# Nodes 4p to 4p+3 of a block on partition p: x and out in runs of 1 KB, turns that read every fourth column, and four changes of order

## The reference

```python
# layer 0: e = par * (diag * x @ W) + x, with one set (u) for nodes 0..2047 and one (i) for the rest
h = adj @ (adj.T @ e)
x = _layernorm(x + (layernorm(h) * gamma + beta + x))
# layer 1
x = _layernorm(x + (1.0 - 0.1 * x - 0.01 * sum(x * (adj @ x), axis=1)))
# layer 2
deg = clip(sum(adj, axis=1) + 1.0, 1.0, None)
z = concatenate([x, (adj @ x + x) / deg]) @ W + b
x = _layernorm(x + relu(z) / max(norm(relu(z)), 1e-12))
# layer 3
T1 = L @ x; T2 = 2 * L @ T1 - x; T3 = 2 * L @ T2 - T1      # L is adj
x = _layernorm(x + x @ w[0] + T1 @ w[1] + T2 @ w[2] + T3 @ w[3] + bias)
```

## Time and profile before

| | us |
|---|---|
| median of 3 runs | 1488.62 (1487.05 to 1488.67) |
| the profiled execution, its own time | 1490.14 |
| its span | 1487.5 |
| PE busy | 1471.7 (99%) |
| DVE busy | 612.6 (41%) |
| ACT busy | 257.5 (17%) |
| DMA queue of SP, share of 16 engines | 90.1% |

### The profile page before, as it was taken

The page is one execution under the profiler, slowest core; times in us unless marked ns, Lnnn a source line. Parts: engine busy times, 40 slices in busy tenths (PEclk is TensorE's granted clock), DMA queues, the critical chain, the costliest instruction groups (busy, mean ns, idle before and its releaser), DMA issues.

```text
span 1487.5 us, 17128 instructions
## 1 busy us (share of the span) xinstructions
PE 1471.7 (99%) x6422; PEld 683.8 (46%) x6422; DVE 612.6 (41%) x1274; ACT 257.5 (17%) x535; POOL 61.3 (4%) x66
## 2 busy tenths in 40 slices
PE   8999999999999999999999999999999999999997
PEld 5555555555555543334444344444444434444332
DVE  5756565655555568424222653325111031100532
ACT  3433434343433320000100000100000010000210
POOL 0000000000000002100000011000000000000010
PEclk9999999999999999999999999999999999999999
DMA  9999999999999998999888698776487879888998
GB/s 306 392 414 417 416 414 405 387 415 392 390 416 401 389 397 330 421 420 421 303 296 302 277 365 315 283 269 257 150 287 286 299 295 354 299 301 306 395 421 321
DMA packets 121632, 517.86 MB, mean 348 GB/s; under 512 B 20396, under 2 KB 20436, under 8 KB 71636
## 3 DMA queue, kind: packets, MB, share of 16 engines
q1 hardware_dynamic: 119664, 516.46, 90.1%
q10 hardware_dynamic: 1892, 0.35, 0.1%
HBM read 410.61 MB, written 106.17 MB: 347 GB/s over the span
## 4 chain that ended last, share of the span: by engine, by line
issue 99%; POOLq 0%; POOL 0%; DVE 0%
POOL power_out L541 0%; POOLq L539 0%; POOLq L541 0%; DVE rows L1046 0%; POOL ident L534 0%; POOLq L536 0%; POOL ident L536 0%; POOLq L1308 0%
## 5 line engine op out<-in xcount | busy, mean ns | idle before, releaser
L855 PE MATMUL ps_u<-blk,vectors 128*128 128x512 f32 (+1 forms) x1904 | 681.4, 593 | 1.3 <-DMA blk<-a_transposed 1.1
L855 PEld LDWEIGHTS ps_u<-blk,vectors 128*128 128x128 f32 (+1 forms) x1904 | 274.8, 170 | 368.4 <-issue 362.3
L580 ACT ACTIVATE blk<-ps_turn 128x512 f32<-128x512 f32 x400 | 201.9, 625 | 331.0 <-PE ps_turn L665 317.2
L1222 DVE TENSOR_TENSOR part<-part,ps_u 64x512 f32<-64x512 f32 (+1 forms) x40 | 27.4, 686 | 447.6 <-PE ps_u L855 447.0
L710 PE MATMUL ps_h<-blk,u_rows 128*64 128x512 f32 x720 | 164.4, 599 | 0.0
L957 DVE TENSOR_REDUCE row_part<-blk 128x4 f32<-128x2048 f32 x68 | 152.4, 2278 | 0.1
L941 DVE TENSOR_TENSOR part<-part,ps_h 128x512 f32<-128x512 f32 x80 | 55.0, 687 | 184.3 <-PE ps_h L710 184.3
L693 PE MATMUL ps_u<-blk,e 128*64 128x512 f32 x544 | 125.3, 600 | 0.1
L665 PEld LDWEIGHTS ps_turn<-ident,blk 128*128 128x128 f32 x1040 | 113.5, 141 | 19.5 <-issue 19.5
L665 PE MATMUL ps_turn<-ident,blk 128*128 128x128 f32 x1040 | 120.6, 274 | 0.0
L541 POOL TENSOR_TENSOR power_out<-power_in,minus_half 128x4 f32<-128x4 f32 x60 | 60.6, 1010 | 1422.6 <-DVEq L1009 1422.6
(11 more groups left out here) (119 smaller groups left out, 621.5 us busy)
## 6 DMA issues: line engine op xcount, KB each, us to landing
blk<-a_transposed SPq DMA_DIRECT2D x276, 1024.0 KB, 6.2
a_transposed<-blk SPq DMA_DIRECT2D x100, 1024.0 KB, 13.4
blk<-in_adj SPq DMA_DIRECT2D x65, 1024.0 KB, 11.9
nat_far<-in_adj SPq DMA_DIRECT2D x32, 1024.0 KB, 11.8
early_blk<-a_transposed SPq DMA_DIRECT2D x12, 1024.0 KB, 8.1
blk<-in_adj SPq DMA_DIRECT2D x12, 256.0 KB, 6.3
nat_far<-a_transposed SPq DMA_DIRECT2D x2, 1024.0 KB, 12.1
rows<-in_x SPq DMA_DIRECT2D x10, 128.0 KB, 8.2
```

The source lines that it names most:

```text
L580: nc.scalar.activation(blk[:, n % RING, t, :], ps_t[t][:, :], ACT.Copy)\
L855: mm = pe.matmul(acc, left, tiles[:, t, :], start=first, stop=last)
L1222: V.tensor_tensor(part[parts, cols], part[parts, cols], ps_both[r % 2][parts, :], ALU.add)\
```

## The change

Partition p now holds nodes 4p to 4p+3 of a block, tile c node 4p + c. x and out then lie in memory as one run of 1 KB per partition and block, where they were four of 256 bytes. A tile of adj is still 128 runs of 2 KB, but the four of a partition are neighbouring rows. So that a turned block has its contraction in the same order, the transposes of adj and of u (`every_fourth`) read 128 columns that lie 16 bytes apart. diag comes as 10 rows of 512, is multiplied by par on its 10 partitions before it is turned, and par goes to those 10 partitions only. The order changes in these places: x of block 1 is loaded and turned after the first quarter of block 1; first_e goes behind the third quarter; times_w(1) goes ahead of u_part(0); e(1) is made ahead of the first row sum; W_i is issued one block later; turn_h(3), (7) and (9) and the addition for e = 3 go earlier; diagonal blocks in sweep 4 go ahead of the last block of row 6; the addition of (5, 4) goes into the root wait of row 3.

```diff
-    a_blocks = adj.rearrange("(t p) j -> p t j", p=P)
-    x_rows = x.rearrange("(t p) f -> p t f", p=P)
-    out_rows = out.rearrange("(t p) f -> p t f", p=P)
+    a_blocks = adj.rearrange("(i p c) j -> p i c j", p=P, c=TB)
+    x_rows = x.rearrange("(i p c) f -> p i c f", p=P, c=TB)
+    out_rows = out.rearrange("(i p c) f -> p i c f", p=P, c=TB)
...
+    RUN_BEFORE_END = {2: HEAD[2] + 2, 4: 6}
+    SOON_TURNED, SOON_ADDED = {(1, 1): 3}, {0: 1, 1: 3}
+    TURNED_TWO = (6, 8)
...
-                    if s == LATE_HEAD and r == head + 2:
+                    if r == RUN_BEFORE_END.get(s):
...
+        def every_fourth(row, t):
+            return row.rearrange("p (q t) -> p t q", t=TB)[:, t, :]
...
-                if n < NB:
-                    tiles = slice(n * TB, (n + 1) * TB)
-                    sp.dma_start(rows[:, tiles, :], x_rows[:, tiles, :]).then_inc(x_loaded[n], 16)
+                tiles = slice(n * TB, (n + 1) * TB)
+                if n < NB and n != 1:
+                    sp.dma_start(rows[:, tiles, :], x_rows[:, n]).then_inc(x_loaded[n], 16)
                 if n < IN_QUARTERS:
                     for c in range(TB):
-                        sp.dma_start(nat(n)[:, c, :], a_blocks[:, n * TB + c, 0:BLK])\
+                        if n == 1 and c == 1:
+                            sp.dma_start(rows[:, tiles, :], x_rows[:, n]).then_inc(x_loaded[n], 16)
+                        sp.dma_start(nat(n)[:, c, :], a_blocks[:, n, c, 0:BLK])\
...
-            const(diag_flat[0:UT, :], diag_u.rearrange("(t p) -> t p", p=P))
-            const(diag_flat[UT:NT, :], diag_i.rearrange("(t p) -> t p", p=P))
+            const(diag_flat[0:UB, :], diag_u.rearrange("(i q) -> i q", q=BLK), diag_loaded)
+            const(par[0:UB, :], par_u.partition_broadcast(UB), diag_loaded)
+            const(diag_flat[UB:NB, :], diag_i.rearrange("(i q) -> i q", q=BLK), diag_loaded)
+            const(par[UB:NB, :], par_i.partition_broadcast(NB - UB), diag_loaded)
             for h in range(2):
                 const(w0[half(h), 0, h, :], w_u)
-            const(par[:, 0, :], par_u.partition_broadcast(P), par_u_loaded)
-            const(par[:, 1, :], par_i.partition_broadcast(P), par_i_loaded)
...
-                        mm = pe.transpose(ps_t[t][:, c * P:(c + 1) * P], nat(n)[:, c, t * P:(t + 1) * P],
+                        mm = pe.transpose(ps_t[t][:, c * P:(c + 1) * P], every_fourth(nat(n)[:, c, :], t),
                                           ident[:, :])
...
-                    mm = pe.transpose(ps_u[j % 2][:, t * P:(t + 1) * P], u_turned[:, t * P:(t + 1) * P], ident[:, :])
+                    mm = pe.transpose(ps_u[j % 2][:, t * P:(t + 1) * P], every_fourth(u_turned[:, :], t), ident[:, :])
...
             def first_u():
+                times_w(1)
                 u_part(0)
-                times_w(1)
 
             turn_x_in(0)
-            turn_quarters(0, {1: first_e})
-            turn_x_in(1)
-            turn_quarters(1, {1: first_u})
+            turn_quarters(0, {2: first_e})
+            turn_quarters(1, {0: lambda: turn_x_in(1), 1: first_u})
...
-                if e > 0:
+                if e > 0 and e not in SOON_TURNED.values() and e - 1 not in TURNED_TWO:
                     turn_h(e)
+                    if e in TURNED_TWO:
+                        turn_h(e + 1)
...
-            def weigh_diag(k, tiles):
-                V.tensor_tensor(par_prod[:, k:k + 1], par[:, k, 0:1], par[:, k, 1:2], ALU.mult)
-                dve.drain()
+            def weigh_diag():
+                dve.wait_ge(diag_loaded, 16 * N_DIAG)
+                V.tensor_tensor(par_prod[:, :], par[:, 0:1], par[:, 1:2], ALU.mult)
+                dve.drain()
+                V.tensor_scalar(diag_flat[:, :], diag_flat[:, :], par_prod[:, 0:1], None, ALU.mult)
+                dve.drain().then_inc(diag_weighed, 1)
                 dve.wait_ge(diag_turned, 1)
-                V.tensor_scalar(diag[:, tiles], diag_in[:, tiles], par_prod[:, k:k + 1], None, ALU.mult)
+                V.tensor_copy(diag[:, :].rearrange("p (i c) -> p c i", c=TB),
+                              diag_in.rearrange("p (c i) -> p c i", c=TB))
                 dve.drain()
...
+                if soon is not None:
+                    soon()
                 V.tensor_tensor(out_rows_centred[r % 2][:, :, :], ta[:, :, :], over_rows(mean_var[:, :, 0]), ALU.subtract)
...
-                if e + 2 < NB:
+                if e + 2 < NB and e + 2 not in SOON_ADDED.values():
                     add_last_h(e + 2)
...
+                        elif s == SWEEPS - 1 and r == 3:
+                            ENDS[s](i, n, soon=lambda: add_y(s, 4))
```

More of the change, by code:

```diff
@@ L112, in build @@
         w3_copy = sb("w3_copy", [P, F])
-        diag_flat = sb("diag_flat", [NT, P])
+        diag_flat = sb("diag_flat", [NB, BLK])
         diag = sb("diag", [P, NT])
-        par = sb("par", [P, 2, 2])
-        par_prod = sb("par_prod", [P, 2])
+        par = sb("par", [NB, 2])
+        par_prod = sb("par_prod", [NB, 1])
         vec = sb("vec", [P, 4, F])
@@ L527, in _ @@
                 i = at(SWEEPS - 1, r)
[L528 removed]
+                sp.dma_start(out_rows[:, i], rows[:, i * TB:(i + 1) * TB, :])\
                     .then_inc(stored, 16)
@@ L634, in turn_diag @@
             def turn_diag():
-                pe.wait_ge(consts_loaded, 16 * N_CONSTS)
-                pe.matmul(diag_in, diag_flat[:, :], ident[0:NT, 0:NT], start=True, stop=True)\
-                    .then_inc(diag_turned, 1)
+                pe.wait_ge(diag_weighed, 1)
+                for c in range(TB):
+                    mm = pe.matmul(diag_in[:, c * NB:(c + 1) * NB], every_fourth(diag_flat[:, :], c),
+                                   ident[0:NB, 0:NB], start=True, stop=True)
+                mm.then_inc(diag_turned, 1)
             def turn_x_in(i):
@@ L898, in _ @@
                         last_h_part(SOON_H[blocks[b][1:3]])
+                    if blocks[b][1:3] in SOON_TURNED:
+                        turn_h(SOON_TURNED[blocks[b][1:3]])
                     multiply_block(b)
```

28 lines of the change are left out of this document (12 added, 16 removed).

## The result

| | before | with the change |
|---|---|---|
| median | 1488.64 us (4 runs) | 1507.09 us (4 runs, 1506.95 to 1508.18) |
| span of the profiled execution | 1487.5 us | 1505.2 us |
| loads of a turn, mean time of one | 141 ns | 209 ns |
| the turn of block 2 starts at | 22.16 us | 21.76 us |
| the last turn starts at | 1480.22 us | 1498.17 us |

The ratio is 1.0126, 95% interval 1.0114 to 1.0139: slower by 1.3%, where 1484.5 us and a range up to 1493 had been forecast. Something costs about 20 us, and the rest of the change gives back about 2.

What follows compares the result with a forecast made beforehand. The prediction took PE's instruction count and spacing as the bound, with PE never idle from 30 to 540 us. Terms +1.1 - 4.0 - 1.0 - 0.2 = -4.1 us gave a median of 1484.5 us, range 1479.5 to 1493.

Steps and rivals of the forecast that it cites:

- Step 1: Turns of adj and u: strided loads move the rhythm from 109 to 110 ns, +1.1 us; upper bound +189 us.
- the first rival: Turns of adj and u: load becomes PE's rhythm, each turn paying its reading beyond 109 ns, mostly 1500 to 1680; chance 0.20.
- The witness: Loads of L655 read for 106 ns yet start 110 ns apart, so a load may take twice as long in the background.
- Step 2: Start up to block 2's turn: fewer transfer runs and new order bring it near 17.5 us, not 22.16; claimed -4.0 us.
- the start does not shorten: Start: W and diag late, block 1's quarters late, or clock falls; gain 0 to 1.5 us, median 1486 to 1489; chance 0.20.
- its third condition: At the start, the granted clock falls again, leaving a gain there of only 0 to 1.5 us.
- Step 3: Later order: e = 3's addition -0.8 us, sweep 4's diagonal blocks -0.2, the 0.45 us near 1414 us counted 0; together -1.0 us.
- Step 4: Last store of out: 128 runs instead of 512 make it shorter, -0.2 us, between 0 and -0.5.

Runs made afterwards that it cites:

- a2_diag: The changed kernel with contiguous turns of adj and u, and the four turns of diag contiguous too; 1484.0 us (one run).
- a1_contiguous: The changed kernel with turns of adj and u reading 128 neighbouring columns again; 1487.31 us (10 runs), ratio 0.9987 to the kernel before.
- the first probe: The kernel before with thirteen groups of 24 products at various steps behind block 0's turn, each group reading the same columns; no total time given.

## Why the prediction was wrong

**Step 1, the strided turns, failed, and it alone made the sign wrong.** It said that a load may take twice as long in the background, took 112 ns of reading, and concluded that "the rhythm goes from 109 to 110 ns, 1640 x 0.7 ns = +1.1 us". Measured are loads of 209 ns and a rhythm of 120, so the term is 20 us, not 1.1. The mechanism was the first rival's, the load as PE's rhythm, deciding from 1.9 times the present reading time as said there (2.2 times by the same split, 124 ns against 56), and 1507 us lies in its 1500 to 1680. Its arithmetic is only near: 124 - 109 = 15 ns, 1640 times, would be 24.6 us, and 20 were found, so the split into 85 fixed ns and reading puts the size a fifth too high. What was wrong was the choice between the ends. The witness, L655's loads with 106 ns of reading at 110 ns apart, is a load of another kind; it was taken to say what a strided turn costs, though it says only what a contiguous ordinary load costs. And the margin I gave it, 3 ns in 109, multiplied by 1640, decided the case: a value of 112 with bounds of 56 and 224 should have put far more than 0.20 beyond 109. With 20.1 us in place of 1.1 the sum would have given 1503.5 us; most of the other 3.6 us is the start's.

**Step 2, the start: -4.0 forecast, -0.4 found.** The transfers did as forecast: no wait for x, DMA share 0.94, diag's turn at 7.63 us and the product with W without a wait behind it. Four small turns, "0.7 us" in the sum, took 2.0 us because they are ordinary products with a step, and x of block 1, forecast for 11.3 us, came at 13.23. But most of the term was the clock. The forecast set a start at the full level against a profile with a spell of 3.2 us at the lower one, and gave 0.6 us back. The unchanged start has no such spell in some executions (block 2's turn at 18.93 and 19.07 us), so these 3.2 us were not the change's to gain: at a like clock it gains 0.4 to 0.6 us. And filling PE's idle time didn't keep the clock up: it fell at about 9.9 us behind 5 us of work without a gap. That is the rival "the start does not shorten", by its third condition. a2_diag, free of the spell and of the strided diag, reached block 2's turn at 18.57 us, 3.6 us earlier than the profile of before and 1.1 later than the 17.5 forecast.

**Step 3, the order later: -1.0 forecast, about -2.1 found,** with the pieces wrong both ways. For the addition for e = 3 0.8 us were forecast: the wait for DVE moved to the next addition (1.11 us at 588.17), and 0.3 us were lost by row 5. The paired turns 7 and 9, which had no term in the sum, gave 0.6 us back, so 0.3 us were gained by 688 us (20.1 to 19.8). The rest, 19.77 - 17.95 = 1.8 us, came from the diagonals (1.3 us, for which 0.2 were counted, and for a wait that stayed) and from the 0.45 us of the addition (5, 4), which nothing takes back once the last loads are in time: I read the 1.1 us of waits for loads as a limit that takes gains back, and did not see that the same edit removes it. That the 0.45 us of the addition (5, 4) is given back when alone fits its one run, and isn't shown by it.

**Step 4, the end: -0.2 forecast, -0.25 found.** Right: from the last turn to the end of the span the three kernels that store out in runs of 1 KB (the changed kernel, a1_contiguous, a2_diag) take 7.03 to 7.09 us, all others 7.27 to 7.35.

Sum: +20.5 for the stride, -0.4 at the start, -0.3, -1.8 and -0.25: 17.7 us of span.

## What to carry to other kernels

When PE has no idle time, a change to how it reads its operands is the first thing to price, because it is multiplied by every instruction; a cover of half the rhythm is no cover once the reading time more than doubles, and the price then has to be measured, with two dozen products in a row, before anything is rebuilt around it. A wait that is removed in a chain paced by another engine comes back at the next place that waits for the same engine, so compare the time at which that engine does its next piece, not the wait. Moving work can be worth more than the wait for which it was moved, here probably because it frees buffers earlier. And a start that runs at two clocks from one execution to the next must be compared at a like clock, or the clock's microseconds are booked as the change's.

## What the runs showed of the hardware

- A turn's weight load of 128 columns in float32 takes 141 ns when contiguous and 194 to 209 ns with each of the steps tried, 2 to 16 elements; turns stand 109 ns apart, and with a step 113 to 114 (steps 3, 8, 16), 118 (step 5) or 119 to 120 (steps 2 and 4). Steps of 2 and 4 being the dearest was not expected, and its cause isn't settled.
- At the lower clock the step of 4 costs a turn nothing that shows: four loads start 0.93 us ahead of the next group with it (13.45 us in the changed kernel) and 0.94 without (13.34 us in a1_contiguous).
- An ordinary float32 product's loads stand 112 ns apart with step 1, 118 with 2 and 233 with 4; the same step of 4 costs a turn 11 ns and an ordinary load 121.
- The granted clock can fall while PE is busy without a gap: to 0.50 at about 9.9 us in the changed kernel, after 5 us of work, and at about 55.8 us in the first probe, during products with 32 moving columns. In the same probe it stood at 1.00 from 10 to 30 us, when PE did next to nothing but turns.
- The clock's spell at the lower level near the start comes and goes between executions of the same kernel and is worth about 3 us here: with one and the same order of the start block 2's turn begins at 22.16, 21.73, 20.95 and 20.54 us with a spell, and at 19.07 and 18.93 us with the clock at 1.00 from 11.6 to 18.2 us.
- Loads of a_transposed near 664 us, where the DMA share is 1.01, are waited for 0 to 1.1 us in kernels that do the same there.
